# One ScalarE exponential of 1024 columns in place of two of 512 for each half's key and query weights

## The reference

```python
def reference(x, ...):
    x = x + _L0_attn_ref(_layernorm(x), ...)
    x = x + _L0_ffn_ref(_layernorm(x), ...)

# attention
q_dists = jnp.sum((q[:, :, :, None, :] - centers[None, None]) ** 2, axis=-1)
k_dists = jnp.sum((k[:, :, :, None, :] - centers[None, None]) ** 2, axis=-1)
q_weights = jnp.exp(q_dists * inv_var)
k_weights = jnp.exp(k_dists * inv_var)
logits = jnp.einsum('bihs,bjhs,hs->bijh', q_weights, k_weights, amplitudes)
attention = jax.nn.softmax(logits / temp, axis=2)
out = jnp.einsum('bijh,bjhd->bihd', attention, v).reshape(Bx, Tx, Dx)
return out @ out_w.T
# feed-forward: r = sigmoid(xr @ W_r); out = r * (square(relu(xk @ W_k)) @ W_v)
```

## Time and profile before

| what | value |
|---|---|
| median of 3 runs | 2180.16 us (2179.97, 2184.02, 2180.16) |
| the profiled execution | 2180.0 us, its span 2178.2 us |
| instructions in the span | 51414 |
| mean granted TensorE clock | 0.998 |

### The profile page before, as it was taken

The page is one execution under the profiler, slowest core; times in us unless marked ns, Lnnn a source line. Parts: engine busy times, 40 slices in busy tenths (PEclk is TensorE's granted clock), DMA queues, the critical chain, the costliest instruction groups (busy, mean ns, idle before and its releaser), DMA issues.

```text
span 2178.2 us, 51414 instructions
## 1 busy us (share of the span) xinstructions
PE 2131.8 (98%) x22372; PEld 961.3 (44%) x22372; DVE 882.9 (41%) x1868; ACT 2012.9 (92%) x2194; POOL 389.6 (18%) x490
## 2 busy tenths in 40 slices
PE   8999999999999999999999999999999999999998
PEld 5434444444444444444444444444444444444445
DVE  5235434344534343444423534442334424423336
ACT  3899999999999999999999999999999999999995
POOL 0244242433202022022130220320300000000001
PEclk9999999999999999999999999999999999999999
DMA  6644544453312414216042332530241131211111
GB/s 177 172 115 134 123 122 113 132 151 105 98 48 66 130 50 120 77 55 163 24 113 91 76 99 72 130 98 24 82 118 42 40 86 50 62 34 34 33 40 50
DMA packets 176470, 193.28 MB, mean 89 GB/s; under 512 B 88640, under 2 KB 108480, under 8 KB 176224
## 3 DMA queue, kind: packets, MB, share of 16 engines
q1 hardware_dynamic: 166960, 174.96, 29.2%
q0 software_dynamic: 7168, 14.69, 2.9%
q10 hardware_dynamic: 2096, 0.14, 0.1%
HBM read 99.03 MB, written 75.94 MB: 80 GB/s over the span
## 4 chain that ended last, share of the span: by engine, by line
PE 80%; ACT 14%; DVE 3%; issue 1%; DMA 1%; SPq 0%; POOL 0%; DVEq 0%; POOLq 0%
PE ps_pv L899 36%; PE ps_scores L880 24%; PE ps_step L927 16%; ACT probs L1222 13%; PE ps_step L950 2%; PE ps_scores L912 1%; ACT weight L1286 1%; PE ps_step L906 1%; PE ps_scores L917 1%; DMA x_ffn<-x 0%; DVE den_all L1731 0%; DVE tmp L1583 0%; DVE mixed_r L1575 0%; PE ps_scores L922 0%; PE ps_scores L921 0%
## 5 line engine op out<-in xcount | busy, mean ns | idle before, releaser
L1222 ACT ACTIVATE probs<-ps_scores 128x1024 f32<-128x1024 f32 x2048 | 1939.8, 1034 | 100.8 <-PE ps_scores L880 75.9
L899 PE MATMUL ps_pv<-probs,vals 128*32 128x512 f32 (+5 forms) x9848 | 1073.9, 529 | 0.1
L880 PE MATMUL ps_scores<-q_aug,k_aug 49*128 49x512 f32 x4096 | 708.1, 441 | 14.6 <-ACT probs L1222 11.4
L880 PEld LDWEIGHTS ps_scores<-q_aug,k_aug 49*128 49x128 f32 x4096 | 332.6, 184 | 618.7 <-ACT probs L1222 561.0
L899 PEld LDWEIGHTS ps_pv<-probs,vals 128*32 128x32 f32 x9848 | 342.8, 139 | 225.7 <-issue 132.5
L1352 POOL DMA_DIRECT2D packed<-qk x224 | 113.1, 511 | 919.2 <-DVE qk L1525 864.8
L1357 POOL TENSOR_TENSOR packed<-qk 32x512 f32<-32x512 f32 x224 | 235.7, 1052 | 16.9
L1592 DVE COPY o_raw<-ps_pv 128x512 f32<-128x512 f32 x64 | 44.3, 692 | 445.9 <-PE ps_pv L899 445.9
L1731 DVE RECIPROCAL den_all<-den_all 128x128 f32<-128x128 f32 x252 | 223.6, 923 | 0.6
L1362 POOL TENSOR_TENSOR k_act<-k_act 128x512 f32<-128x512 f32 x28 | 30.4, 1085 | 788.0 <-DVE k_act L1528 788.0
L1525 DVE COPY qk<-ps_step 128x512 f32<-128x512 f32 x56 | 38.6, 689 | 177.8 <-PE ps_step L927 177.8
(11 more groups left out here) (218 smaller groups left out, 1087.6 us busy)
## 6 DMA issues: line engine op xcount, KB each, us to landing
k_aug<-k_parts SPq DMA_DIRECT2D x128, 192.0 KB, 4.4
q_aug<-q_parts SPq DMA_DIRECT2D x128, 192.0 KB
k_parts<-parts SPq DMA_DIRECT2D x32, 512.0 KB, 3.4
q_parts<-parts SPq DMA_DIRECT2D x32, 512.0 KB, 3.9
packed<-qk POOLq DMA_DIRECT2D x224, 64.0 KB, 2.3
x_ffn<-x SPq DMA_DIRECT2D x18, 512.0 KB, 4.5
k_parts<-parts SPq DMA_DIRECT2D x32, 256.0 KB, 4.2
q_parts<-parts SPq DMA_DIRECT2D x32, 256.0 KB, 4.9
```

Of the source, the lines that this page charges most:

```text
L880: mm = pe.matmul(ps_scores[:, g % RING, e, :], k_aug[rows, s % 2, pair, kt * P:(kt + 1) * P], q_aug[rows, u % 2, pair, :], start=True, sto ...
L899: mm = pe.matmul(ps_pv[32 * c:32 * c + 32, at], vals[:, s % 2, kt, :, c], probs[:, tick % PROB_SLOTS, c, at], start=(kt == 0), stop=(kt == ...
L1222: act.activation(probs[:, tick % PROB_SLOTS, 2 * pair:2 * pair + 2, :], ps_scores[:, g % RING, :, :], ACT.Exp).then_inc(probs_ready, 1)
```

## The change

One ScalarE instruction exponentiates `weight[:, :, :]`, both sides of a half. Its gap is the first after dist_q's last gap, moved on by up to 3 gaps to one with much side work. The key side's split stands two gaps after it, the query side's three. The store of the parts follows two ticks behind the latter, as before. The semaphore `weighted` rises once a half. `load` counts 0.5 for the one exponential.

```diff
-def weigh_gap(task, half, side):
-
-    first = gap_of(end(task, f"dist_{'kq'[side]}{half}")) + 1
-    if side:
-        first = max(first, weigh_gap(task, half, 0) + 2)
+def weigh_gap(task, half):
+
+    first = gap_of(end(task, f"dist_q{half}")) + 1
     return next((gap for gap in range(first, first + WEIGHED_AFTER) if full(gap)), first)
 
 
 def split_tick(task, half, side):
 
-    return name_of(weigh_gap(task, half, side) + 2)
+    return name_of(weigh_gap(task, half) + 2 + side)
...
-WEIGH_AT = beside((weigh_gap(task, half, side), (task, half, side)) for task, half in WEIGHTS for side in range(2))
+WEIGH_AT = beside((weigh_gap(task, half), (task, half)) for task, half in WEIGHTS)
...
-                for task, half, side in WEIGH_AT.get(gap, ()):
-                    act.wait_ge(step_free, STEP_NO[task, f"dist_{'kq'[side]}{half}"] + 1)
-                    act.activation(weight[:, side, :], weight[:, side, :], ACT.Exp, scale=inv_var[:, half:half + 1]).then_inc(weighted, 1)
+                for task, half in WEIGH_AT.get(gap, ()):
+                    act.wait_ge(step_free, STEP_NO[task, f"dist_q{half}"] + 1)
+                    act.activation(weight[:, :, :], weight[:, :, :], ACT.Exp, scale=inv_var[:, half:half + 1]).then_inc(weighted, 1)
...
-                v.wait_ge(weighted, FIRST_EXPS + 2 * WEIGHT_NO[which] + side + 1)
+                v.wait_ge(weighted, FIRST_EXPS + WEIGHT_NO[which] + 1)
```

## The result

The changed kernel takes 2185.85 us (median of 11 runs, 2185.27 to 2189.57), the kernel before 2180.61 us (11 runs). The ratio is 1.0025, 95% interval [1.0017, 1.0033]: slower by 5.2 us. The profiled execution took 2185.3 us, with a span of 2183.5 us against 2178.2.

A forecast was written before the change was run, and what follows sets the result against it. TensorE was taken as the bound, with ScalarE having little to spare. Longer third-group waits, moved slices included, gave +4.3 us, VectorE, SyncE and POOL nothing: 2180.16 + 4.3 = 2184.5 us, range 2178.5 to 2190.0.

The forecast's parts named there:

- the bound of 4.4 us: What a measurement of this kernel can tell from no change, about 0.2%; the forecast of +4.3 us stood on it.
- the mechanism's own part: In the loop's gaps, TensorE's third score groups wait longer for ScalarE's exponentials: +4.3 us in sum, moved slices included.
- The price: On ScalarE, one weight exponential of 1024 columns puts off the next exponential by 1.04 us; one of 512 columns by 0.61.
- The lower bound from the durations: On ScalarE, the delay by a 1024-column weight exponential, worked out from instruction durations: 1.02 us from below.
- The two-gap rule: TensorE's third score group two gaps behind a weight exponential waits unless two gaps last 6.64 us (6.21 for 512 columns).
- Gap 203's wait: Worked example in one half: TensorE's third score group waits 0.49 us there, where two waits together made 0.1 us before.
- the sign of 3 to 5 us more waiting than the 11.4: Expected evidence if right: TensorE's waits for the probabilities rise from 11.4 us by 3 to 5 us.
- ScalarE as the bound: Rival: ScalarE's work sets the time, so the 5.1 us saved come off in full, 2175.1 us; chance 0.09.
- The absorbed delay: Rival: the three-slot ring's 2.8 us covers the 1.04, third groups wait no more in sum, 2180.2 us; chance 0.10.
- VectorE's crowding: Rival: splits closer together push evictions late, adding 3 or 4 waits of 1 us each, 2188.3 us; chance 0.11.
- The wait of 1.07 us that the prediction named: At 1451.07 us in the kernel before, TensorE waited for a VectorE eviction behind a split and two more operations.

## Why the prediction was right

The forecast was 2184.5 us with 0.47 on slower; measured is 2185.85, inside the range, and slower. Same had 0.44: the forecast stood on the bound of 4.4 us, the mechanism's own part measures 4.6 and 4.7, and what carries the medians to 5.2 and 5.7 is not in the prediction.

- **The price.** Taken as 1.04 us from four instructions ahead of the loop; the late ones put off their follower by 1.04 (679.66 to 680.70; 1.04 is also the median of all 28 and the least), though their duration is 1.163 us against 1.146. The lower bound from the durations was of no use, the start of the follower was.
- **The two-gap rule.** Gap 203's wait was worked out as 0.49 us and is 0.56; gap 201 as 2.96 and is 2.96. Gap 202 was worked out as 3.19 and is 3.13: its old wait of 0.05 went, and with it the nearly 0.1 us on top that the rule lacked. Over gaps 4 to 504 the sum was +4.3 and is +4.6 and +4.7.
- **Two terms missed, which cancel.** The third groups' waits rise by 6.1 us (33.0 to 39.1), not by 4.3; those two gaps behind the exponentials are 14.2 us in sum, not 12.3. And the prediction lacked the 0.1 us on top of each wait: 40 gaps lost their wait and with it 3.2 us, 24 gained one and 1.1 us. Fewer gaps wait in the changed kernel, each longer. (By the starts; the profile's 34 places against 19 are only the waits so long that TensorE ran dry.) One of the 24 is gap 455, which is shorter for a reason of VectorE's, below. 6.1 - 2.1 = 4.0 us, and VectorE's new wait of 0.5 us brings it near the 4.6. That the sum came out right to 0.4 us is partly luck. So is the sign of 3 to 5 us more waiting than the 11.4: the +4.4 lacks the 2.1 us wait at the loop's start, and within 100 to 1600 us the rise is 6.0. With 0.1 us for each waiting gap put into the rule afterwards, the case of no exponentials comes out at -10.0 us, where -10.1 was measured.
- **ScalarE as the bound** is excluded: taking all its late weight work away gives 10 us, not 30, and two instructions in one gap are slower than one. The rule of the Trainium skill, page "VectorE: DVE Perf Modes", section "The TRN2 errata", that one large instruction pays the fixed latency once, holds as a price: the merged form is 4.6 us better in the same gap. It was named as the rival by which the time would fall, and the place outweighs it.
- **The absorbed delay** is excluded by the waits, 11.7 us in place of 5.7 within 100 to 1600 us.
- **VectorE's crowding** was priced at -1 to +3 us beside the forecast. Moving the splits is worth +0.5 us, one wait, at 1419 us, and taking it at nothing was right to that extent. The wait of 1.07 us that the prediction named, in gap 455, is 0.63 us in the changed kernel and unchanged with the splits moved alone.
- **No gap for the clock.** The prediction had none, and the profiled execution lost 1.7 us to it and gained 0.7 at the loop's start. The kernel before does the same in other executions.

## What to carry to other kernels

Where two engines hand buffers around a short ring, an instruction slipped into one engine's stream costs what it exceeds the slack of its own stretch: two short ones with a pause between can be cheaper than one long one of less total time. Read the slack as the length of the stretch until the buffer is asked for again minus the engine's work in it, and compare it with the start-to-start price of the new instruction. When such an instruction changes size, the weights by which a schedule balances around it have to change too.

## What the runs showed of the hardware

- A score group that waited for ScalarE at all lengthened the rest of its gap by 0.08 us on average beyond the wait itself (40 gaps without late exponentials, 0.084 each; 40 in the changed kernel, 0.081 each).
- The granted clock fell to 1.2 GHz for 3.4 us behind a wait of 1.5 us near 2080 us in 7 of 12 profiles, in both kernels, and each drop cost 1.4 to 1.7 us. Two profiles had another at the equal wait near 330 us. TensorE was busy 97 or 98% of the span in all of them. So two profiles of one kernel can differ by 1.7 us in a single gap, and a change of a few us is better read gap by gap than from the span.
- An exponential from SBUF of 1024 columns in the loop lasted 1.163 us where the four ahead of it lasted 1.146, but put its follower off by the same 1.04 us.
